# A decoder layer on one core: the attention's weighted sums in two parts, a norm and two casts moved to GpSimd

## The chip, the core and the metric

The kernel runs on one core of one Trainium2 chip. The metric is the device time of one execution in microseconds (us), median of three runs. All matrix products are made by TensorE (PE), from stationary weights that PE loads itself (PEld, beside the matmuls). VectorE (DVE), ScalarE (ACT) and GpSimd (POOL) work on rows of 128 partitions, SyncE (SP) issues the transfers.

## The reference, cut to what matters

For four sequences of 512 tokens of width 512, with a `_layernorm` after each of three parts:

```python
x = _layernorm(x + attn(x))          # 16 heads of 32, rope, causal softmax, then Wo
x = _layernorm(x + xattn(x, ctx))    # attention matrix made from ctx alone, 512x512, applied to x's columns
x = _layernorm(x + ffn(x))           # silu(gate) * up, 512 -> 2048 -> 512
# attn:   scores = q k^T / sqrt(32), causal;  out = softmax(scores) v
# xattn:  query, key = ctx Wq^T + bq, ctx Wk^T + bk (256 -> 128);  energy = query key^T;  x softmax(energy)^T
```

Everything is in float32 precision. Most products are made of three products of rounded halves (a high part `_hi` in the type fp32r and the rest `_lo`): hi x hi, lo x hi, hi x lo.

## The kernel before

The program is written out by engine, and each engine has one loop over the same numbered slots (`for t in range(BEGIN, END)`). What an engine does in slot t, and in which order, is fixed by tables; engines meet only at semaphores.

The attention takes 256 slots: 16 groups (four sequences by four groups of heads), 16 slots each (four heads by four blocks of 128 query rows). In slot t:

- PE makes the scores of tile t (L675, `ps`), then the pieces of other units that the table gives to this slot (`unit`, L660 for products, L658 for transposes: projections q, k, v, the output projection `o`, and from slot 224 on units of the cross attention: `c` context projections, `t` and `a` transposes, `e` energies, `m` mixing), then the transposes of the probabilities of tile t - 3 (L688, into `pa`, `pb`, `pc`).
- DVE takes the row maximum of tile t and writes `prob` (L1164); in other slots it moves `pb` and `pc` to `pT` (`move_b` L1171, `move_c` L1176).
- ACT takes the exponential of tile t (L902) and moves `pa` (`move_a` L909).

Scores of tile t wait for the row maximum of tile t - 2 (two buffers in PSUM); transposes of tile t wait for its exponential, and those into `pa` for the last `move_a`.

Once in a group, in its slot 20 (slots 20, 36, ... 244), and for the last group after the mixing unit `m1`, PE makes the weighted sums of the group (`weighted`, L703): 28 matmuls, each with a stationary block of only 32 columns (`tile_position`), four side by side in the array, which in the trace are 56 records:

```python
for moved in (a_moved, b_moved, c_moved):
    pe.wait_ge(moved, 4 * n + 4)
...
for k, s, count, at in WEIGHTED:
    for r in range(4):
        mm = pe.matmul(pv[D*r:D*r+D, s*P:(s+count)*P], vg[..][:, k, ..], pT[:, r, at*P:(at+count)*P], ..., tile_position=(0, D*r))
```

After it the reciprocals of the row sums are transposed (`r` unit), moved to `heads` by ACT (`move_r` L916) and multiplied in by DVE (`normalize` L1199).

The norm after attention: DVE sums and takes moments (`summed`, `moments`), POOL makes `rstd` and `nmr` (`root1`, L1513 to L1517), ACT applies them to a token tile (`layer_norm`, L922, `res<-res,nmr,rstd`). There are 16 token tiles, four in a batch (sequence). For a unit of the cross attention's context projection, ACT moves the result and adds the bias (`context_move`, L936), ACT casts its high half (`context_cast`, L941, `cqk_hi`), and POOL takes the low half (`context_query`, L1536, `cqk_lo`); the energies `e` wait for it. The table `CROSS` gives the first units of the cross attention their slots and PSUM banks; `hop` says how many slots behind the unit each step of its follow-up stands on the other engines. So a unit `a` (transposes of attention rows, L658 `pj<-ident,e`) in slot t has its `att_hi` on ACT (L952) in slot t + 1 and its `att_lo` on DVE (L1236) in slot t + 2, behind that slot's exponential, row maximum and moves.

After slot 256 the rest of the cross attention and the feed-forward part follow, which take from about 390 us to the end.

Of the kernel before, what the change touches and what calls it, by code (L numbers as in the profile page):

```python
# [18 lines left out]
ALU = mybir.AluOpType  # L19
# [8 lines left out]
ST = S // P  # L28
# [3 lines left out]
TILES = 16  # L32
# [13 lines left out]
GROUPS = B * G  # L46
# [7 lines left out]
AV, RECIPS, NORMALIZE, SPLIT_O = 20, 21, 25, 26  # L54
# [6 lines left out]

CROSS = [(("c", 0), 224, (6,), 0), (("c", 1), 228, (6,), 0), (("t", 0), 232, (4,), 1), (("e", 0), 234, (3,), 0),
# [3 lines left out]
CHAINS = ("m0:0 c2:3 c3:4 m1:1 AV r15:0 t4:5 t5:6 m2:7 e4:3 e5:4 m3:0 e6:1 e7:2 c4:5 c5:6 t6:7 t7:3 a4:4 a5:0 o12:1 a6:2 a7:5 o13:6 "  # L66
# [78 lines left out]
LAST_AV = ENDS["m", 1] + 1  # L145
# [11 lines left out]
def hop(key, k):  # L157

    return ENDS[key] + HOPS[key[0]][ENDS[key] >= SCORES][k]
# [7 lines left out]
def program(nc, ctx, d, out):  # L167
# [11 lines left out]
    with ExitStack() as first:  # L179
# [13 lines left out]
        res = sb("res", [P, ST, E], F32, first)  # L193
        oT_hi, oT_lo = sb("oT_hi", [P, G, S], F32R, first), sb("oT_lo", [P, G, S], F32R, first)
        o, rb = sb("heads", [P, S], F32, first), sb("rb", [P, ST, 4, D], F32, first)
# [62 lines left out]

    WEIGHTED = [(0, 0, 1, 6), (0, 1, 1, 8), (1, 1, 1, 9), (0, 2, 2, 0), (1, 2, 2, 2), (2, 2, 2, 4), (3, 3, 1, 7)]


    const_in, late_in = sem("const_in"), sem("late_in")
# [288 lines left out]
    def _(pe):  # L553
# [134 lines left out]
                mm = pe.transpose(dst[:, c:c + P], prob[:, t % PROBS, k * P:(k + 1) * P], ident[:])  # L688
            mm.then_inc(t_done, 1)

        def weighted(n):
            for moved in (a_moved, b_moved, c_moved):
                pe.wait_ge(moved, 4 * n + 4)
            pe.wait_ge(v_done, ST * (n // G) + ST)
            if n:
                pe.wait_ge(o_done, n)
            for key in BANKS[2]:
                if 0 < TILES * n + AV - STARTS[key] < TILES:
                    emptied(pe, key)
            for k, s, count, at in WEIGHTED:  # L700
                for r in range(4):
                    c = n % G * P + D * r
                    mm = pe.matmul(pv[D * r:D * r + D, s * P:(s + count) * P], vg[n // G % 2][:, k, c:c + D],  # L703
                                   pT[:, r, at * P:(at + count) * P], start=(k == 0), stop=(k == s + count - 1),
                                   tile_position=(0, D * r))
            mm.then_inc(av_done, 1)

        def three(dst, n, stationary, moving, first=True, final=True):

# [6 lines left out]
        for t in range(BEGIN, END):  # L716
            if 0 <= t < SCORES:
                scores(t)
            for key, start, counts, _ in UNITS:
                if start <= t < start + len(counts):  # L720
                    unit(key, sum(counts[:t - start]), counts[t - start])
            if 0 <= t - LAG < SCORES:
                transposes(t - LAG)
            for n in range(GROUPS):
                if t == (TILES * n + AV if n < GROUPS - 1 else LAST_AV):
                    weighted(n)

# [103 lines left out]
        h, c = NH - 1, NH // 2 - 1  # L831
# [26 lines left out]
    def _(act):  # L858
# [59 lines left out]
        def layer_norm(n):  # L918

            s = n % ST  # L920
            act.wait_ge(nmr_done, n + 1)
            act.activation(res[:, s, :], res[:, s, :], ACT.Identity, bias=nmr[:, s:s + 1], scale=rstd[:, s:s + 1]).then_inc(x1_done, 1)  # L922

        def context_half(b):
# [134 lines left out]
        for t in range(BEGIN, END):  # L1059
# [12 lines left out]
                    if t == ENDS["qk"[u], n] + SPLIT_QK:  # L1072
                        split_qk(n, u)
            for n in range(B * ST):
                if t == hop(("o", n), 3):
                    layer_norm(n)
            for (n, k), (at, _) in SPLIT_W.items():
                if t == at:
# [15 lines left out]
            for key in CONTEXT:  # L1094
                if key[0] == "c" and t == hop(key, 0):
                    context_move(key[1])
                if key[0] == "c" and t == hop(key, 1):
                    context_cast(key[1])
                if key[0] in "ta" and t == hop(key, 0):
                    t_half(*key)  # L1100
                if key[0] == "u" and t == hop(key, 0):
                    pair_input(key[1])
# [359 lines left out]
    def _(pool):  # L1462
# [46 lines left out]
        def root1(n):  # L1509

            s = n % ST
            pool.wait_ge(mv_done, n + 1)
            pool.tensor_scalar(veps[:, s:s + 1], mv[:, s, 1:2], EPS, None, ALU.add).then_inc(veps_done, 1)  # L1513
            pool.wait_ge(veps_done, n + 1)
            pool.tensor_tensor(rstd[:, s:s + 1], veps[:, s:s + 1], mhalf[:], ALU.pow).then_inc(rstd_done, 1)
            pool.wait_ge(rstd_done, n + 1)
            pool.tensor_scalar(nmr[:, s:s + 1], mv[:, s, 0:1], rstd[:, s:s + 1], -1.0, ALU.mult, ALU.mult).then_inc(nmr_done, 1)  # L1517

        def context_rest(b):
# [12 lines left out]
        def context_query(n):  # L1532

            hi, lo = cqk[n // 2 % 2]
            pool.wait_ge(cqkhi_done, n + 1)
            pool.tensor_tensor(lo[:, n % 2, :], c_raw[n // 2 % 2][:, n % 2, :], hi[:, n % 2, :].bitcast(F32),  # L1536
                               ALU.subtract).then_inc(cqklo_done, 1)
# [100 lines left out]
        for t in range(BEGIN, END):  # L1638
# [19 lines left out]
            if t >= 0 and b < B and at == (58 if b == B - 1 else 52):  # L1658
                residual(b)
            for key in CONTEXT:  # L1660
                if key[0] == "c" and t == hop(key, 2):
                    context_query(key[1])
                if key[0] == "e" and key[1] < KT and t == hop(key, 2):
                    energy_scale(key[1])
                if key[0] == "m" and key[1] < 2 * ST and t == hop(key, 1):
                    root(key[1])
# [82 lines left out]
```

## Time and profile before

| | |
|---|---|
| median of 3 runs | 970.6 us (970.26 to 971.39) |
| the profiled execution, its time | 968.91 us |
| its span, first to last instruction | 967.1 us |
| mean granted TensorE clock | 0.994 |
| busy: PE / PEld | 929.7 us (96%) / 756.2 us (78%) |
| busy: DVE / ACT / POOL | 733.9 (76%) / 514.9 (53%) / 598.2 us (62%) |

The profile's rows name an instruction by engine, source line, operation and `out<-in` tiles. A value in brackets is the time the engine sat idle just before it, and what ended that. Matmuls overlap each other in the rows: a 512-column matmul has 0.39 us, and the next one starts 0.23 us after it. Times are counted from the first instruction.

### The profile page before, as it was taken

What the parts mean: (1) busy time and instruction counts of PE and PEld (TensorE: products, weight loads), DVE (VectorE), ACT (ScalarE), POOL (GpSimd) and SP (SyncE); (2) the same over time, 40 slices, a digit from 0 to 9 for tenths busy, and PEclk for the clock granted to TensorE, in tenths of its full rate; (3) what the DMA queues carried; (4) which work ended last, traced back from release to release, by engine and by line L of the source; (5) the groups of instructions that cost most, each with busy time, mean ns of one, the idle gap of its engine ahead of it and who ended that gap; (6) DMA issues with size and microseconds to landing.
All of it is one profiled execution on the core that took longest, in us unless ns stands there. A gap on an engine that the chain in (4) does not pass through costs nothing.

```text
span 967.1 us, 16196 instructions
## 1 busy us (share of the span) xinstructions
PE 929.7 (96%) x5272; PEld 756.2 (78%) x5272; DVE 733.9 (76%) x1589; ACT 514.9 (53%) x1150; POOL 598.2 (62%) x645
## 2 busy tenths in 40 slices
PE   7888999999999978999999999999999999999997
PEld 5666888888788856887888888888878888888885
DVE  5667778678877876779478888867877888777777
ACT  4577777777877776566144443433534354333333
POOL 2467646745875546457466676777846786665644
PEclk9999999999999999999999999999999999999999
DMA  6986666965767780013102101111111113211102
GB/s 221 257 200 167 183 182 163 266 163 143 215 181 197 200 267 1 23 44 115 60 0 67 65 33 66 54 45 66 33 41 58 55 45 109 88 55 66 34 33 88
DMA packets 40883, 105.20 MB, mean 109 GB/s; under 512 B 4960, under 2 KB 5344, under 8 KB 38752
## 3 DMA queue, kind: packets, MB, share of 16 engines
q1 hardware_dynamic: 40800, 104.16, 36.7%
q8 instruction: 44, 0.72, 0.3%
q14 instruction: 39, 0.32, 0.1%
HBM read 78.98 MB, written 25.17 MB: 108 GB/s over the span
## 4 chain that ended last, share of the span: by engine, by line
PE 77%; DVE 6%; POOL 6%; ACT 5%; DMA 3%; issue 3%; SPq 0%; POOLq 0%; DVEq 0%; ACTq 0%
PE pd L712 27%; PE pj L660 14%; PE pj L712 10%; PE pg L712 5%; PE pu L712 5%; PE pv L703 3%; PE ps L675 3%; PE pa L688 2%; PE pb L688 2%; POOL raw L1466 1%; POOL raw L1475 1%; PE pc L688 1%; ACT e L946 1%; POOL raw L1471 1%; DMA qk_scratch<-raw 1%
## 5 line engine op out<-in xcount | busy, mean ns | idle before, releaser
L902 ACT ACTIVATE prob<-prob,nmax 128x512 f32<-128x512 f32 (+3 forms) x256 | 143.8, 562 | 72.9 <-DVE nmax L1164 71.8
L1164 DVE CUSTOM_DVE_ANT_0 prob<-ps,mask 128x512 f32<-128x512 f32 (+3 forms) x256 | 124.2, 487 | 72.5 <-PE ps L675 67.1
L675 PE MATMUL ps<-ks,qs 128*128 128x256 f32 (+2 forms) x256 | 104.9, 411 | 7.0 <-DVE nmax L1164 5.3
L1466 POOL TENSOR_TENSOR raw<-raw,cos 128x512 f32<-128x512 f32 x32 | 42.3, 1323 | 92.1 <-DVE pj L1146 76.5
L1633 POOL TENSOR_TENSOR g_lo<-gated,g_hi 128x512 fp32r<-128x512 f32 x32 | 46.3, 1448 | 79.7 <-ACT g_hi L1006 79.7
L1302 DVE TENSOR_TENSOR xb<-pd,xb 128x512 f32<-128x512 f32 x116 | 79.3, 684 | 19.6 <-PE pd L712 19.3
L1626 POOL TENSOR_TENSOR wop_lo<-wsum,wop_hi 128x512 fp32r<-128x512 f32 x64 | 81.6, 1299 | 1.4 <-ACT wop_hi L991 1.4
L712 PE MATMUL pd<-dn_hi,g_hi 128*128 128x512 f32 x244 | 75.4, 390 | 0.3 <-DVE x3T_lo L1250 0.3
L712 PE MATMUL pd<-dn_hi,g_lo 128*128 128x512 f32 x244 | 75.1, 389 | 0.0
L712 PE MATMUL pd<-dn_lo,g_hi 128*128 128x512 f32 x244 | 75.1, 389 | 0.0
L1606 POOL TENSOR_TENSOR wsum<-f_raw 128x256 f32<-128x256 f32 x32 | 23.7, 742 | 77.9 <-DMA f_raw<-in_w_ffn 77.7
L1006 ACT CAST g_hi<-gated 128x512 fp32r<-128x512 f32 x32 | 19.9, 622 | 91.0 <-DVE gated L1362 91.0
L991 ACT CAST wop_hi<-wsum 128x1024 fp32r<-128x1024 f32 x32 | 33.7, 1055 | 64.9 <-POOL wsum L1611 64.9
L675 PEld LDWEIGHTS ps<-ks,qs 128*128 128x128 f32 x256 | 48.8, 190 | 17.7 <-DVE nmax L1164 7.7
L660 PE MATMUL pj<-xT_hi,w_hi 128*128 128x512 f32 x128 | 51.9, 405 | 5.2 <-ACT xT_hi L872 5.1
L1475 POOL TENSOR_TENSOR raw<-raw,qk_hi 128x512 fp32r<-128x512 f32 x32 | 42.4, 1324 | 18.9 <-ACT qk_hi L896 18.9
L712 PEld LDWEIGHTS pd<-dn_hi,g_hi 128*128 128x128 f32 x244 | 45.6, 188 | 10.5 <-issue 0.7
L712 PEld LDWEIGHTS pd<-dn_hi,g_lo 128*128 128x128 f32 x244 | 45.8, 188 | 9.6
L712 PEld LDWEIGHTS pd<-dn_lo,g_hi 128*128 128x128 f32 x244 | 45.8, 188 | 9.5
L660 PE MATMUL pj<-xT_hi,w_lo 128*128 128x512 f32 x128 | 51.6, 403 | 1.5 <-DVE w_lo L1121 1.5
L660 PE MATMUL pj<-xT_lo,w_hi 128*128 128x512 f32 x128 | 51.4, 401 | 0.6 <-POOL xT_lo L1490 0.6
L688 PE MATMUL pb<-ident,prob 128*128 128x128 f32 x256 | 49.1, 274 | 0.1
(525 smaller groups left out, 2825.3 us busy)
## 6 DMA issues: line engine op xcount, KB each, us to landing
f_raw<-in_w_ffn SPq DMA_DIRECT2D x32, 768.0 KB, 4.2
qs<-qk_scratch SPq DMA_DIRECT2D x64, 256.0 KB, 4.8
ks<-qk_scratch SPq DMA_DIRECT2D x60, 256.0 KB, 7.3
qk_scratch<-qk_hi SPq DMA_DIRECT2D x32, 256.0 KB, 2.1
qk_scratch<-raw SPq DMA_DIRECT2D x32, 256.0 KB, 2.3
res<-in_x SPq DMA_DIRECT2D x4, 1024.0 KB, 5.0
x_scratch<-res SPq DMA_DIRECT2D x4, 1024.0 KB, 6.5
xb<-x_scratch SPq DMA_DIRECT2D x4, 1024.0 KB, 5.8
```

Source lines behind the costliest of these rows:

```text
L660: mm = pe.matmul(over[at], *pairs[i], start=i == 0, stop=i == len(pairs) - 1)
L675: pe.matmul(ps[:, t % 2, 0:w], qs[n % 2][:, r, s * P:(s + 1) * P], ks[n % 2][:, r, 0:w], start=True, stop=True).then_inc(s_done, 1)
L688: mm = pe.transpose(dst[:, c:c + P], prob[:, t % PROBS, k * P:(k + 1) * P], ident[:])
L712: mm = pe.matmul(dst, stationary(k)[a], moving(k)[c], start=(first and part == 0 and k == 0), stop=(final and part == 2 and k == n - 1))
L902: act.activation(prob[:, t % PROBS, 0:w], prob[:, t % PROBS, 0:w], ACT.Exp, bias=nmax[:, n % 2, i:i + 1], scale=-1.0, accum_out=rsum[:, n ...
L991: act.copy(wop_hi[h % 2][:, 3:7, :], wsum[:]).then_inc(wophi_done, 1)
L1164: dve.tensor_tensor_reduce(prob[:, t % PROBS, 0:w], ps[:, t % 2, 0:w], mask[:, S - w:S], -D ** -0.5, 3e38, ALU.add, ALU.min, accum_out=nma ...
L1302: dve.tensor_tensor(tile, pd[:, 2 + n % 2, :], tile, ALU.add).then_inc(part_added, 1)
L1466: pool.tensor_tensor(raw[:, u, :], raw[:, u, :], cos[:], ALU.mult).then_inc(cos_done, 1)
L1475: pool.tensor_tensor(raw[:, u, :].bitcast(F32R), raw[:, u, :], qk_hi[:, u, :].bitcast(F32), ALU.subtract).then_inc(qklo_done, 1)
L1626: pool.tensor_tensor(lo[:, 3 + k:5 + k, :], wsum[:, k:k + 2, :], hi[:, 3 + k:5 + k, :], ALU.subtract).then_inc(woplo_done, 1)
L1633: pool.tensor_tensor(lo, (gated, gated_b)[b][:], hi.bitcast(F32), ALU.subtract).then_inc((glo_done, glo_b_done)[b], 1)
```

## The change

Four edits:

1. `weighted` is cut in two. `weighted_ahead` stands at the end of the slot before (slot 19 of the group) and makes the first two entries of a reordered list, 8 matmuls of 256 columns; it waits for `a_moved` and `b_moved`, the values and the bank. `weighted` waits for `c_moved` and makes the other 20, in the slot in which all 28 stood. For the last group nothing stands between the two.
2. The unit `a0` goes from slot 243 to slot 244.
3. For batch 2 (token tiles 8 to 11), POOL applies the norm itself, with one instruction on 128x512 (`subtract`, `mult`) in `root1`, in the place of its `nmr`; ACT's `layer_norm` for these tiles is gone.
4. For context units 0 and 1, POOL casts the high half in `context_query`, which stands one slot earlier; ACT's cast is gone.

```diff
 CROSS = [...
-         (("e", 3), 241, (3,), 1), (("a", 0), 243, (4,), 0), ...
+         (("e", 3), 241, (3,), 1), (("a", 0), 244, (4,), 0), ...
...
-    WEIGHTED = [(0, 0, 1, 6), (0, 1, 1, 8), (1, 1, 1, 9), (0, 2, 2, 0), (1, 2, 2, 2), (2, 2, 2, 4), (3, 3, 1, 7)]
+    WEIGHTED = [(0, 2, 2, 0), (1, 2, 2, 2), (2, 2, 2, 4), (3, 3, 1, 7), (0, 0, 1, 6), (0, 1, 1, 8), (1, 1, 1, 9)]
...
-        def weighted(n):
-            for moved in (a_moved, b_moved, c_moved):
-                pe.wait_ge(moved, 4 * n + 4)
+        def weighted_ahead(n):
+            pe.wait_ge(a_moved, 4 * n + 4)
+            pe.wait_ge(b_moved, 4 * n + 4)
             pe.wait_ge(v_done, ST * (n // G) + ST)
             if n:
                 pe.wait_ge(o_done, n)
             for key in BANKS[2]:
                 if 0 < TILES * n + AV - STARTS[key] < TILES:
                     emptied(pe, key)
-            for k, s, count, at in WEIGHTED:
+            weighted_part(n, WEIGHTED[:2])
+
+        def weighted(n):
+            pe.wait_ge(c_moved, 4 * n + 4)
+            weighted_part(n, WEIGHTED[2:]).then_inc(av_done, 1)
+
+        def weighted_part(n, part):
+            for k, s, count, at in part:
...
-            mm.then_inc(av_done, 1)
+            return mm
...
             for n in range(GROUPS):
+                if t == (TILES * n + AV if n < GROUPS - 1 else LAST_AV) - 1:
+                    weighted_ahead(n)
                 if t == (TILES * n + AV if n < GROUPS - 1 else LAST_AV):
                     weighted(n)
...
         def layer_norm(n):
...
-            act.wait_ge(nmr_done, n + 1)
+            act.wait_ge(nmr_done, n + 1 - (ST if n >= 3 * ST else 0))
...
-                if t == hop(("o", n), 3):
+                if n // ST != 2 and t == hop(("o", n), 3):
                     layer_norm(n)
...
-                if key[0] == "c" and t == hop(key, 1):
+                if key[0] == "c" and key[1] >= 2 and t == hop(key, 1):
                     context_cast(key[1])
...
             pool.wait_ge(rstd_done, n + 1)
+            if n // ST == 2:
+                pool.tensor_scalar(res[:, s, :], res[:, s, :], mv[:, s, 0:1], rstd[:, s:s + 1], ALU.subtract, ALU.mult).then_inc(x1_done, 1)
+                return
...
             hi, lo = cqk[n // 2 % 2]
+            if n < 2:
+                pool.wait_ge(cqk_moved, n + 1)
+                pool.tensor_copy(hi[:, n, :], c_raw[0][:, n, :]).then_inc(cqkhi_done, 1)
             pool.wait_ge(cqkhi_done, n + 1)
...
-                if key[0] == "c" and t == hop(key, 2):
+                if key[0] == "c" and t == hop(key, 1 if key[1] < 2 else 2):
                     context_query(key[1])
```

PE in slots 242 to 244 (group 14), `pv` the bank of the weighted sums, `pj<-ident,e` the unit `a0`; `ps<-ks,qs` 128x256 is the scores of slot 243, 128x512 those of 244, 128x384 those of 245. Before:

```order
L675 MATMUL ps<-ks,qs 128x256
L658 MATMUL pj<-ident,e 128x128 x4
L688 MATMUL pa<-ident,prob 128x128 x4
L675 MATMUL ps<-ks,qs 128x512
L688 MATMUL pb<-ident,prob 128x128 x3
L703 MATMUL pv<-pT,vg 32x128 x12
L703 MATMUL pv<-pT,vg 32x256 x12
L703 MATMUL pv<-pT,vg 32x128 x4
L675 MATMUL ps<-ks,qs 128x384
```

and now:

```order
L675 MATMUL ps<-ks,qs 128x256
L688 MATMUL pa<-ident,prob 128x128 x4
L710 MATMUL pv<-pT,vg 32x256 x8
L675 MATMUL ps<-ks,qs 128x512
L658 MATMUL pj<-ident,e 128x128 x4
L688 MATMUL pb<-ident,prob 128x128 x3
L710 MATMUL pv<-pT,vg 32x256 x4
L710 MATMUL pv<-pT,vg 32x128 x16
L675 MATMUL ps<-ks,qs 128x384
```

Eight of the weighted sums' matmuls now stand between the transposes of slot 243 and the scores of slot 244, the other 20 where all 28 stood, and `a0` stands behind the scores of slot 244 and no longer ahead of slot 243's transposes. In groups 0 to 13 the same cut is made, without an `a0`.

ACT in slots 244 to 246; `att_hi` is the high half of `a0`, L902/L911 the exponential and L909/L918 the move of `pa`. Before:

```order
L902 ACTIVATE prob,rsum<-prob,nmax 128x512
L932 CAST c_hi<-c_raw 128x1024
L952 CAST att_hi<-pj 128x4x128
L902 ACTIVATE prob,rsum<-prob,nmax 128x384
L909 COPY pT<-pa 128x4x128
L902 ACTIVATE prob,rsum<-prob,nmax 128x128
```

and now:

```order
L911 ACTIVATE prob,rsum<-prob,nmax 128x512
L941 CAST c_hi<-c_raw 128x1024
L911 ACTIVATE prob,rsum<-prob,nmax 128x384
L918 COPY pT<-pa 128x4x128
L961 CAST att_hi<-pj 128x4x128
L911 ACTIVATE prob,rsum<-prob,nmax 128x128
```

`att_hi` of `a0` went from ahead of slot 245's exponential to behind it and behind the move of `pa`.

POOL in slots 225 to 228; `cqk` is context unit 0, the three rows ahead of it belong to token tile 10, and `oT` to the heads of group 12. Before:

```order
L1513 TENSOR_SCALAR veps<-mv 128x1
L1515 TENSOR_TENSOR rstd<-veps,mhalf 128x1
L1517 TENSOR_SCALAR nmr<-mv,rstd 128x1
L1536 TENSOR_TENSOR cqk_lo<-c_raw,cqk_hi 128x512
L1484 CAST oT_hi<-heads 128x512
L1486 TENSOR_TENSOR oT_lo<-heads,oT_hi 128x512
```

and now:

```order
L1522 TENSOR_SCALAR veps<-mv 128x1
L1524 TENSOR_TENSOR rstd<-veps,mhalf 128x1
L1527 TENSOR_SCALAR res<-res,mv,rstd 128x512
L1549 CAST cqk_hi<-c_raw 128x512
L1551 TENSOR_TENSOR cqk_lo<-c_raw,cqk_hi 128x512
L1493 CAST oT_hi<-heads 128x512
L1495 TENSOR_TENSOR oT_lo<-heads,oT_hi 128x512
```

The one-column `nmr` became the whole norm of a tile, and the cast stands ahead of `cqk_lo`.

## Rows read from the trace of the kernel before

**Rows 1.** busy time by stretch: us, PE, PEld, DVE, ACT, POOL, PEclk, DMA, GB/s

```profile
110.00:338.00 228.00, 227.53 (x1732) 185.32 (x1731) 179.77 (x565) 173.63 (x475) 140.56 (x138) 1.00 0.69 185
338.00:380.00 42.00, 32.30 (x269) 24.02 (x268) 30.25 (x95) 31.57 (x88) 24.39 (x21) 0.96 0.49 157
376.00:379.00 3.00, 2.92 (x9) 2.16 (x9) 1.37 (x4) 2.42 (x7) 2.17 (x2) 0.50 0.01 3
```

**Rows 2.** timeline of PE at group 6's weighted sums; start, us

```profile
187.75 0.49 PE L688 MATMUL pb<-ident,prob 128*128 128x128 f32 x3
188.18 2.38 PE L703 MATMUL pv<-pT,vg 128*32 128x128 f32 x56
190.48 0.45 PE L675 MATMUL ps<-ks,qs 128*128 128x384 f32 x1
190.76 0.39 PE L660 MATMUL pj<-xT_hi,w_hi 128*128 128x512 f32 x1
```

**Rows 3.** timeline of PEld there

```profile
188.17 2.11 PEld L703 LDWEIGHTS pv<-pT,vg 128*32 128x32 f32 x56 [0.17 <-issue]
190.48 0.19 PEld L675 LDWEIGHTS ps<-ks,qs 128*128 128x128 f32 x1 [0.20 <-issue]
```

**Rows 4.** timeline of PE, the same passage with no weighted sums between

```profile
94.45 0.49 PE L688 MATMUL pb<-ident,prob 128*128 128x128 f32 x3
...
94.95 0.39 PE L660 MATMUL pj<-wv_hi,xT_hi 128*128 128x512 f32 x1
```

**Rows 5.** instructions of L703 there: x, duration ns min/median/max, forms

```profile
L703 PE MATMUL pv<-pT,vg x56: 272/285/379, 188.2 to 190.3; 128*32 128x128 f32 x32, 128*32 128x256 f32 x24
```

**Rows 6.** timeline of PE behind group 1's weighted sums

```profile
87.18 0.50 PE L660 MATMUL pj<-xT_lo,w_hi 128*128 128x512 f32 x1 [0.37 <-POOL xT_lo L1490]
```

**Rows 7.** timeline of PE behind group 13's weighted sums

```profile
342.78 0.63 PE L688 MATMUL pa<-ident,prob 128*128 128x128 f32 x4 [0.92 <-ACT pT L909]
...
346.11 0.47 PE L660 MATMUL pj<-cqk_hi 128*128 128x512 f32 x1 [0.58 <-POOL cqk_lo L1536]
```

**Rows 8.** timeline of ACT there

```profile
343.97 0.63 ACT L941 CAST cqk_hi<-c_raw 128x512 fp32r<-128x512 f32 x1
...
344.99 0.81 ACT L922 ACTIVATE res<-res,nmr,rstd 128x512 f32<-128x512 f32 x1
...
346.40 0.61 ACT L902 ACTIVATE prob<-prob,nmax 128x384 f32<-128x384 f32 x1
```

**Rows 9.** timeline of DVE there

```profile
345.34 0.56 DVE L1164 CUSTOM_DVE_ANT_0 prob<-ps,mask 128x384 f32<-128x384 f32 x1 [0.96 <-PE ps L675]
```

**Rows 10.** timeline of POOL, a cast and a scaling of 128x512

```profile
346.57 0.61 POOL L1484 CAST oT_hi<-heads 128x512 fp32r<-128x512 f32 x1 [0.61 <-DVE heads L1199]
...
352.73 1.59 POOL L1542 TENSOR_SCALAR e<-e,erec 128x512 f32<-128x512 f32 x1 [4.18 <-DVE erec L1226]
```

**Rows 11.** timeline of PE around group 14's weighted sums

```profile
360.00 0.66 PE L658 MATMUL pj<-ident,e 128*128 128x128 f32 x4 [1.51 <-ACT e L946]
...
361.86 2.38 PE L703 MATMUL pv<-pT,vg 128*32 128x128 f32 x56 [0.21 <-issue]
364.16 0.44 PE L675 MATMUL ps<-ks,qs 128*128 128x384 f32 x1
...
365.87 0.65 PE L658 MATMUL pj<-ident,e 128*128 128x128 f32 x4 [0.22 <-DVE att_lo L1236]
```

**Rows 12.** timeline of ACT there

```profile
358.70 0.56 ACT L909 COPY pT<-pa 128x512 f32<-128x512 f32 x1
...
364.16 0.58 ACT L952 CAST att_hi<-pj 128x512 fp32r<-128x512 f32 x1
...
365.86 0.57 ACT L909 COPY pT<-pa 128x512 f32<-128x512 f32 x1
```

**Rows 13.** timeline of DVE there

```profile
361.23 0.42 DVE L1176 COPY pT<-pc 128x256 f32<-128x256 f32 x1
...
365.13 0.69 DVE L1236 TENSOR_TENSOR att_lo<-pj,att_hi 128x512 fp32r<-128x512 f32 x1
```

2 rows, old and new, of the table CROSS are left out of this document.

## Prediction

> **What bounds the kernel now.** I read busy time by stretch first. From 110 to 338 us, the dense part of the attention, PE is busy 227.53 of 228 us [rows 1]: nothing on DVE, ACT or POOL can win anything there, and whatever is added to PE is paid in full. From 338 to 380 us, where the first units of the cross attention stand among the last attention slots, PE is busy 32.30 of 42 us [rows 1]: 9.7 us of idle time, which only there something can give back. So the cut of the weighted sums, which is made in every group, is judged in the dense stretch, and what is taken off ACT in the other one.
>
> The timelines of PE and PEld at one group's weighted sums show what such a visit costs. The 56 records end without a gap inside, but PEld idles 0.17 us before the first weights and 0.20 us before the weights of the scores behind them, ended by no other engine [rows 3]. In all other places of this passage PEld loads ahead, beside the matmuls. The sum of starts agrees: from the transposes ahead to the product behind, 190.76 - 187.75 = 3.01 us [rows 2]; without a visit the same passage takes 94.95 - 94.45 = 0.50 us [rows 4]. The visit takes 2.51 us. Its columns need less: one record of 256 columns is 379 - 272 = 107 ns longer than one of 128 [rows 5], four run side by side, and 56 records are 14 quartets, 8 of 128 and 6 of 256 columns, 20 blocks of 128: 2.14 us. Left are 0.37 us of going into the 32-column form and out of it.
>
> **The change part by part.**
>
> *The cut, in the dense stretch.* It moves 8 of 28 matmuls a slot ahead and adds no matmul. It adds a second way in and out per group. The price of one pair lies between 0.20 us (only the gap behind is of the form, the gap ahead belongs to the semaphores waited for, of which the second part has one instead of several) and 0.37 us (both gaps). I take 0.35, near the upper end, since both gaps stand in PEld with no releaser and the columns' account leaves as much. The Trainium skill (TensorEngine Tiling (Array Packing), Key Properties) states that changing the tiling mode drains TensorE; by that rule both parts pay both gaps, and this term would be 11 x 0.37 = +4.1 us; where the gap ahead is the waits', it would be 11 x 0.20 = +2.2 us. Does the cut remove a wait in exchange? In the dense stretch there is none to remove: PE idles 0.47 us in 228.
>
> It is paid in groups 0 to 12, 13 times, less twice: behind group 1's weighted sums PE waits 0.37 us for `xT_lo` [rows 6], a chain of a transfer, an ACT cast and a POOL subtraction which began before; the same wait comes once more, behind group 9's. There the added 0.35 disappears in the wait. 11 x 0.35 = +3.85 us; with 0.20 +2.2, with 0.37 +4.1.
>
> *The norm of tiles 8 and 9 on POOL* falls in the dense stretch. ACT is busy 173.63 of 228 us there and not waited for: 0. On POOL one instruction of 128x512 with a scalar per row takes 1.59 us [rows 10] in place of a small one. POOL is busy 140.56 of 228 us [rows 1], which covers it; without that cover the queries and keys of group 15 would come up to 1.6 us late per tile.
>
> *Tiles 10 and 11 and the two casts* stand around 338 us. ACT loses the casts (0.63 us each) and two norms (0.81 each) [rows 8]. Those of tile 10 and unit 0 lie ahead of group 13's weighted sums, where ACT idles afterwards: 0. Behind them ACT is what PE waits for [rows 7], and 0.63 + 0.81, some 1.2 us because consecutive ACT instructions overlap a little, leave its queue. It can't use all: its exponential at 346.40 needs a row maximum that ends at 345.34 + 0.56 = 345.90, and that waited 0.96 us for PE [rows 8, 9]. So 0.50 us come forward, less the 0.35 that group 13's own second pair puts ahead of everything: about -0.1 net, from where the shape of before goes on. POOL's path to `cqk_lo` replaces an ACT cast, between other ACT work, by its own of 0.61 us [rows 10], right behind the moved unit; the wait of 0.58 us at 346.11 [rows 7] goes. What is late next there is `x1T_lo` on DVE, behind the same ACT chain. If nothing of the ACT relief came through, this part would be +0.35; if all of it, -1.2 + 0.35 = -0.85.
>
> *Group 14 and `a0`.* Before, `a0` waits to 360.00 for ACT's exponential of the energies, and slot 243's transposes and slot 244's scores queue behind it; then the weighted sums wait to 361.86 for DVE's `c` copy (361.23 + 0.42) [rows 11, 13]. Now the transposes can go at 358.70 + 0.56 = 359.3 [rows 12], and the first part (four blocks of 256 columns over two passes, 8 x 0.107 = 0.86, and 0.35) fills the hole up to about 360.9, where the scores of slot 244 stood before. `a0` (0.44) and the transposes (0.33) follow, and the second part starts without a wait at 362.1. The scores of slot 245 start at 363.5 instead of 364.16 [rows 11]: -0.65.
>
> But who waits for `a0`? Before, its `att_hi` stood on ACT at 364.16, ahead of slot 245's exponential; `att_lo` followed at 365.13 and ended at 365.82, and `a1` started at 365.87 [rows 11 to 13]. Now `att_hi` stands behind slot 245's exponential and behind the move of `pa`, both of which hang on the scores of slot 245. Before, that move ended at 365.86 + 0.57 = 366.43, 2.27 us after the scores started [rows 11, 12]; now at 363.5 + 2.3 = 365.8. `att_hi` ends at 366.3 to 366.4, `att_lo` (0.69) at 367.05, `a1` starts at 367.15 instead of 365.87: +1.3. Queued behind `a1` on PE are transposes into `pa` and the scores of slot 248, on DVE behind `att_lo` the row maximum of slot 247. The transposes had a small wait of their own behind `a1`, so a little less, I take +1.1, arrives at the scores of slot 248, and in front of the next waits nothing gives it back. From 0 (the delay falls into the waits that follow) to +1.3; the +1.1 stays.
>
> *Group 15* has no slot between its parts: only the order of its blocks changes, 0. The norm's and casts' other consequences (the store of batch 2 a little earlier) are waited for by nobody.
>
> **The sum:** +3.85 - 0.1 + 1.1 = +4.85 us on the profiled execution's own 968.9 us (span 967.1), that is 973.8. The median of the runs shown is 970.6, 1.7 above that execution; I add the difference to the median: **975.5 us**. With the ends of each term the sum goes from 2.2 - 0.85 + 0 = +1.35 to 4.1 + 0.35 + 1.3 = +5.75.
>
> **The rivals.** 0.2% is 1.9 us, about what a measurement of this kernel can tell from no change.
>
> *B, the second pair is (nearly) free.* The gaps could belong to the semaphores and the record keeping, and the second part could load its first weights beside the transposes. For it speaks only that no releaser is named; against it the columns' account. Time: 970.6 + 1.0 = 971.6, no change.
>
> *C, faster: the stall-rich stretch closes.* Place: 338 to 380 us, 9.7 us of PE idle. There each engine waits in turn for the last, so an earlier ACT and a second part that no longer waits could return at every later wait and not once. It has to give back 3.85 + 1.9 = 5.8 of the 9.7 us before the kernel is faster. With three quarters, 7.3: 970.6 + 3.85 - 7.3 = 967.2. Against it: of the listed waits the first two alone are ACT's casts and norms, and `a0`'s new place lengthens a chain.
>
> *D, TensorE's clock.* The granted clock is 0.50 from 376 to 379 us [rows 1], 1.2 instead of 2.4 GHz, behind the passage with the waits. PE is busy 2.92 us there; at full clock it would need half. One more such fall, or that one gone: 1.4 us either way, 976.9 or 974.1.
>
> *E, the change doesn't do what it says:* the first part could wait for `b_moved` in its slot. In group 14 `pb`'s copy is due before the hole ends, and elsewhere it comes before the next transposes; I give it no chance of its own.
>
> **How the numbers follow.** Forecast 0.60, its own range 973.5 to 977.5. B 0.12. C 0.08. D 0.20, half each way, both slower than before. So slower 0.80, same 0.12, faster 0.08. The range leaves out C and small tails: 971.0 to 978.0, from B and the lower ends of the terms to a clock fall on top.
>
> **What would show it.** Right: two visits of L710 in PE in each group 0 to 14, with 8 and 20 matmuls, and twice as many idle gaps of PEld of about 0.2 us before `pv` and before `ps`; a group in the dense stretch about 0.35 us longer from one weighted sum to the next; `cqk_lo` no longer waited for; the scores of slot 245 earlier relative to group 13's, but `a1` later behind them. Wrong: PEld without the second pair of gaps, or PE's idle time in the stretch of the crossover down from 9.7 us by more than 4.

## The result, and the profile after

| | before | after |
|---|---|---|
| median | 970.46 us (7 runs, 968.75 to 971.39) | 976.63 us (7 runs, 974.33 to 978.77) |
| ratio | | 1.0063, 95% interval 1.0047 to 1.0079 |
| profiled execution, its time / span | 968.91 / 967.1 us | 976.63 / 974.8 us |
| mean granted TensorE clock | 0.994 | 0.995 |
| busy: PE / PEld | 929.7 / 756.2 us | 934.4 / 756.1 us |
| busy: DVE / ACT / POOL | 733.9 / 514.9 / 598.2 us | 729.3 / 511.5 / 606.1 us |

The change made the kernel slower by 6.1 us (4.6 to 7.7), where 4.9 were forecast. PE has 4.7 us more busy time with the same matmuls. Part of it is that the profile counts the time around the weighted sums as busy (227.34 of 228 us in the dense stretch below); part can be the clock, for the run further down with all 28 matmuls in one piece has 933.1 us without any cut.

Busy time by stretch after (us; PE, PEld, DVE, ACT, POOL; granted clock; DMA; GB/s), for [rows 1]:

```profile
110.00:338.00 228.00, 227.34 (x1717) 181.90 (x1716) 176.27 (x555) 170.13 (x468) 140.57 (x133) 1.00 0.67 178
338.00:380.00 42.00, 34.79 (x277) 27.09 (x275) 29.71 (x96) 28.46 (x81) 24.39 (x22) 0.92 0.63 203
360.00:364.00 4.00, 3.99 (x16) 3.60 (x17) 3.93 (x14) 2.83 (x10) 2.14 (x2) 0.57 0.89 352
374.00:377.00 3.00, 3.00 (x15) 2.82 (x14) 0.82 (x3) 0.96 (x3) 0.00 (x0) 0.50 0.00 0
```

PE is as full in the dense stretch as before, but its records there are 1717 where they were 1732: it is slower, not idle. Between 338 and 380 us its idle time fell from 9.7 to 7.2 us, but that is no gain: the work in this window has moved by 6 us, and two stretches at half clock stand there (before one), in which four transposes into `pa` are busy 1.06 us instead of 0.60.

PE after, at group 6's weighted sums (start, us), for [rows 2]:

```profile
190.12 0.60 PE L688 MATMUL pa<-ident,prob 128*128 128x128 f32 x4
190.65 1.07 PE L710 MATMUL pv<-pT,vg 128*32 128x256 f32 x16
191.65 0.50 PE L675 MATMUL ps<-ks,qs 128*128 128x512 f32 x1
...
192.69 0.49 PE L688 MATMUL pb<-ident,prob 128*128 128x128 f32 x3
193.11 1.51 PE L710 MATMUL pv<-pT,vg 128*32 128x256 f32 x40
194.55 0.44 PE L675 MATMUL ps<-ks,qs 128*128 128x384 f32 x1
```

And PEld, for [rows 3]:

```profile
190.65 0.59 PEld L710 LDWEIGHTS pv<-pT,vg 128*32 128x32 f32 x16 [0.17 <-issue]
191.65 0.19 PEld L675 LDWEIGHTS ps<-ks,qs 128*128 128x128 f32 x1 [0.41 <-issue]
...
193.10 1.24 PEld L710 LDWEIGHTS pv<-pT,vg 128*32 128x32 f32 x40 [0.17 <-issue]
194.55 0.19 PEld L675 LDWEIGHTS ps<-ks,qs 128*128 128x128 f32 x1 [0.20 <-issue]
```

Both parts have a gap ahead and a gap behind. The gap behind the first part reads 0.41 and not 0.20 us. The blocks that end there have 256 columns, and PE may still be at work on them when PEld has loaded their weights; that is argued, not shown. A dearer change of form it is not, as the sum of starts shows. From the first record to the next instruction the two parts take 191.65 - 190.65 = 1.00 and 194.55 - 193.11 = 1.44 us. Before, all 56 records took 190.48 - 188.18 = 2.30 us [rows 2], so the two parts take 0.14 us more. The rest of the price is ahead of the added visit: the transposes into `pa` start 0.53 us before it (190.12 to 190.65), where before they started 0.36 us ahead of the scores:

```profile
186.38 0.60 PE L688 MATMUL pa<-ident,prob 128*128 128x128 f32 x4
186.74 0.48 PE L675 MATMUL ps<-ks,qs 128*128 128x512 f32 x1
```

These are 0.17 us; 0.14 + 0.17 = 0.31, and from one group to the next 0.33 are measured.

**Where the time went.** Each matmul of PE was set against the same one before, and the shift between them followed from the start:

- 1.7 us are there at 45 us, ahead of the first weighted sums. The change does not touch what stands ahead of that, and every other traced execution is late there too against this one of before, by 0.6 to 1.8 us, with a cut or without. So this is a matter of the single execution that was profiled.
- From group 0 to group 12 the shift grows at each weighted sum, by 0.33 us in most: the scores behind the sums stand at 86.79 instead of 84.54 in group 1 (+2.25), at 194.55 instead of 190.48 in group 6 (+4.07), at 301.55 instead of 296.26 in group 11 (+5.29). The period of a group is 301.55 - 280.15 = 21.40 us, before 296.26 - 275.19 = 21.07. 13 such steps are 4.3 us. In these two executions they come to 3.95: 0.37 are lost once behind group 9, in a wait for `xT_lo`, 0.17 around 75 us, where before has a fall of the clock and after has none, and 0.14 are added by a longer wait behind group 1.
- Between groups 12 and 13, a new stall: the shift goes up by 0.77.
- Group 13 adds 0.36, the energies' wait for `cqk_lo` gives 0.69 back.
- The next transposes into `pa`, which hang on ACT, take 0.23 of these 0.69 again: the shift behind them is 6.32.
- Around group 14 the shift rises by 1.41, to the end. `a1` is 1.26 later than what comes in. In the run with tiles 8 and 9 normed on ACT, where no fall of the clock stands near, 1.03 of the same 1.26 last (3.77 us of shift ahead, 4.80 behind). The other 0.38 are the clock: the falls at 360 and 374 us after against the one at 376 before.

1.7 + 3.95 + 0.77 + 0.36 - 0.69 + 0.23 + 1.41 = 7.7 us, the difference of the spans.

The wait behind group 9 is nothing that a cut takes in. Of the 13 executions with a trace only that of the kernel before has it:

```profile
256.13 0.50 PE L660 MATMUL pj<-xT_lo,w_hi 128*128 128x512 f32 x1 [0.21 <-POOL xT_lo L1490]
```

In the run of the new order in one piece, without a cut, the same product starts at 255.90 with no wait. So the cut costs its 0.33 us in each of the 13 groups, 4.3 us, and against an execution without that wait and with the clock set aside the terms are 4.3 + 0.77 - 0.10 + 1.03 = 6.0 us; the medians say 6.1.

The new stall: PE waits for the move of `pa`.

```profile
326.64 0.63 PE L688 MATMUL pa<-ident,prob 128*128 128x128 f32 x4 [0.40 <-ACT pT L918]
```

The exponential ahead of that move, and the move, on ACT:

```profile
325.32 0.61 ACT L911 ACTIVATE prob<-prob,nmax 128x384 f32<-128x384 f32 x1 [2.73 <-DVE nmax L1173]
...
325.93 0.56 ACT L918 COPY pT<-pa 128x512 f32<-128x512 f32 x1
```

The row maximum for which the exponential waits, on DVE, and what stands ahead of it:

```profile
321.94 2.02 DVE L1202 COPY rb<-rrec 128x512 f32<-128x512 f32 x1
...
324.72 0.56 DVE L1173 CUSTOM_DVE_ANT_0 prob<-ps,mask 128x384 f32<-128x384 f32 x1
```

POOL at that time:

```profile
318.00 2.10 POOL L1527 TENSOR_SCALAR res<-res,mv,rstd 128x512 f32<-128x512 f32 x1
...
321.30 2.38 POOL L1541 TENSOR_TENSOR c_lo<-c_raw,c_hi 128x1024 fp32r<-128x1024 f32 x1
```

Read from the bottom: the norm of token tile 8, the first of the four on POOL, takes 2.10 us, so `c_lo` starts only at 321.30, behind one more subtraction, and runs when DVE's copy of the reciprocals, `rb`, is issued. The copy takes 2.02 us, the row maximum behind it is late, and so are the exponential and the move.

### The profile page after: what moved, and what is told of

Its sections match the earlier page's. It is cut to its first block, busy times and chain, and to the rows that moved or that the text cites. A ratio compares the mean times of both kernels' runs of the same rounds, so it can differ in the third digit from the quotient of the medians.

```text
span 974.8 us, 16190 instructions
## 1 busy us (share of the span) xinstructions
PE 934.4 (96%) x5272; PEld 756.1 (78%) x5272; DVE 729.3 (75%) x1589; ACT 511.5 (52%) x1144; POOL 606.1 (62%) x647
## 4 chain that ended last, share of the span: by engine, by line
PE 78%; DVE 6%; ACT 5%; POOL 4%; DMA 3%; issue 2%; SPq 0%; POOLq 0%; DVEq 0%; ACTq 0%
PE pd L719 27%; PE pj L660 14%; PE pj L719 10%; PE pg L719 5%; PE pu L719 5%; PE ps L675 4%; PE pv L710 4%; PE pa L688 2%; PE pb L688 2%; POOL raw L1475 1%; DMA qk_scratch<-raw 1%; PE pc L688 1%; ACT e L955 1%; PE pj L658 1%; POOL raw L1480 1%
## 5 line engine op out<-in xcount | busy, mean ns | idle before, releaser
L911 ACT ACTIVATE prob<-prob,nmax 128x512 f32<-128x512 f32 (+3 forms) x256 | 143.8, 562 | 84.1 <-DVE nmax L1173 83.2
```

The lines of the kernel that those rows point to most:

```text
L911: act.activation(prob[:, t % PROBS, 0:w], prob[:, t % PROBS, 0:w], ACT.Exp, bias=nmax[:, n % 2, i:i + 1], scale=-1.0, accum_out=rsum[:, n ...
```

## The experiments

All were timed in rounds beside runs of the kernel before on the same chip. Ratios are to those.

### Two theories and what would tell them apart

One theory is the prediction's: each further visit to the 32-column form costs a pair of gaps, about 0.33 us, whatever it waits for, and around group 14 the new place of `a0` costs. The rivals: the cost comes of the order of the blocks or of the wait in the middle; the cost comes of the work moved to POOL; the cut in group 14 costs and not `a0`.

### The cut alone, groups 0 to 13

```diff
+    CUT = (0, 1, 2, 3, 4, 5, 6, 7, 8, 9, 10, 11, 12, 13)
...
+                if n in CUT and t == TILES * n + AV - 1:
+                    weighted_ahead(n)
```

> The kernel before with the cut alone, in groups 0 to 13 (group 14 and a0 as before, no work moved to POOL). Theory (each way into and out of the 32-column form costs 0.33 us of PE, as the trace after shows from one group to the next): 13 groups in the dense stretch less one or two absorbed in the wait for xT_lo, 0 to 0.35 for group 13: +3.7 to +4.4 us. Rival (the cut is free, the 6 us come from POOL's work and from group 14): +0.5 us or less.

Measured: 975.43 us, ratio 1.0055 (1.0034 to 1.0076): +5.3 us (3.3 to 7.4). In its trace the period of a group is 278.96 - 257.56 = 21.40 us as in the changed kernel. The growth per group is 0.31 to 0.35 us. Its span is 4.4 us longer than that of before, but 1.3 of them stand there at 45 us; the shift grows by 3.15 us up to group 12, since behind groups 1 and 9 the waits for `xT_lo` of that one execution are missing here (0.5 and 0.37 us). They are missing without a cut too: up to the same place five uncut kernels (the moves to POOL twice, tiles 10 and 11 with the casts, the new order in one piece, group 14 and `a0`) win 1.0 to 1.2 us on that execution. Against them the cut costs 4.1 to 4.3 us, 13 times 0.32 to 0.33. The cut alone makes most of the whole difference of 6.1.

### A third visit per group

Against the kernel of the cut alone:

```diff
             pe.wait_ge(c_moved, 4 * n + 4)
-            weighted_part(n, WEIGHTED[2:]).then_inc(av_done, 1)
+            weighted_part(n, WEIGHTED[3 if n in CUT else 2:]).then_inc(av_done, 1)
...
+            for n in CUT:
+                if t == TILES * n + AV:
+                    weighted_part(n, WEIGHTED[2:3])
             if 0 <= t - LAG < SCORES:
                 transposes(t - LAG)
```

> As the run with the cut in groups 0 to 13, with a third visit in each of these groups (the third entry alone, ahead of slot 20's transposes). Nothing else moves. Theory (a visit costs 0.33 us of TensorE however small its part): one group to the next 21.7 us in the dense stretch, against 21.07 before and 21.4 with two parts; +8 to +9.5 us against before. Rival (the cost is of the slot in which the first part stands, or of the semaphores): a third part behind the same semaphores adds nothing, +5 us as with two parts.

Measured: 979.1 us, ratio 1.0096 (1.0078 to 1.0115), +9.3 us (7.5 to 11.1) for two further visits in 14 groups, 28 visits: 0.33 us each. The period is 284.08 - 262.39 = 21.69 us, 0.62 over that of before, 0.31 per visit. PEld at group 6, the middle part:

```profile
195.26 0.16 PEld L713 LDWEIGHTS pv<-pT,vg 128*32 128x32 f32 x8 [0.37 <-issue]
195.83 0.31 PEld L689 LDWEIGHTS pb<-ident,prob 128*128 128x128 f32 x3 [0.41 <-issue]
```

The middle part waits for nothing that the first had not waited for, and has both gaps all the same. The price goes with the number of visits, not with their length and not with their waits.

### The new order with a wait in the middle, but in one piece

```diff
+    CUT = ()
...
+        def weighted(n):
+            if n not in CUT:
+                weighted_ahead(n)
+            pe.wait_ge(c_moved, 4 * n + 4)
+            weighted_part(n, WEIGHTED[2:]).then_inc(av_done, 1)
```

> The kernel before with the new order of the blocks and with the wait for c_moved between block 2 and 3, but all 28 matmuls in one slot, in all groups. Theory (the price is of changing form, not of waiting): 2.31 us from the first weighted sum to the scores behind, as before, and 0 us in all (within 0.2%). Rival (the semaphore wait in the middle is the price): +0.2 us or more a group, +3 us.

`weighted_ahead` waits for `a_moved` and `b_moved` and makes the first two blocks, as in the change. Measured: 970.03 us, ratio 0.9995 (0.9982 to 1.0008). PE and PEld at group 6:

```profile
188.26 2.38 PE L713 MATMUL pv<-pT,vg 128*32 128x256 f32 x56
```

```profile
188.26 2.11 PEld L713 LDWEIGHTS pv<-pT,vg 128*32 128x32 f32 x56 [0.17 <-issue]
190.56 0.19 PEld L676 LDWEIGHTS ps<-ks,qs 128*128 128x128 f32 x1 [0.20 <-issue]
```

The same 2.38 and 2.11 us as before, in another order and with a wait between. The 56 records stand without a gap inside, so the semaphore was there when it was waited for: neither the order nor such a wait costs anything that can be measured.

### Only the moves to POOL, twice

`weighted` and `a0` stay as before; of the change only these two parts are made, with ACT's instructions gone:

```diff
+            if n in (8, 9, 10, 11):
+                pool.tensor_scalar(res[:, s, :], res[:, s, :], mv[:, s, 0:1], rstd[:, s:s + 1], ALU.subtract, ALU.mult).then_inc(x1_done, 1)
+                return
...
+            if n in (0, 1):
+                pool.wait_ge(cqk_moved, n + 1)
+                pool.tensor_copy(hi[:, n, :], c_raw[0][:, n, :]).then_inc(cqkhi_done, 1)
```

> The kernel before with the norm of batch 2 and the casts of context units 0 and 1 on POOL, no cut. Theory 1 (ACT's relief is worth 0.1 to 0.5 us behind group 13, and the row copy on DVE that POOL's longer queue now holds up costs 0.5 us behind group 12): between -0.3 and +0.4 us. Theory 2 (relief closes idle time at every later wait of the stretch): -1.2 us or better.

Measured: 968.91 us, ratio 0.9989 (0.9976 to 1.0001). The trace shows the energies' wait for `cqk_lo` gone, which brings their start forward by 0.70 us; 0.22 go again at the next transposes into `pa`, and 0.48 last. There is no new stall at 320 us. Since this was the fastest of all, it was run again:

> The kernel before with only the two moves to POOL (norm of tiles 8 to 11, casts of units 0 and 1), a second time and beside the kernels of this call. Theory 1: the wait for cqk_lo goes and 0.8 us come back, 969.6 us, ratio 0.9985 to 0.9995. Theory 2: the first run's 0.9989 was chance, ratio 0.9995 to 1.0010.

Measured: 970.47 us, ratio 1.0000 (0.9988 to 1.0012). In the trace 0.69 us come back at the same place and 0.46 last; in the time nothing is left that can be told from no change. No version was found that beats the kernel before.

### The moves to POOL in parts

First only the norm of tiles 8 to 11 (the first piece of the diff above). Then the norm of tiles 10 and 11 with the two casts: `if n in (10, 11)` in the first piece, and the second piece.

> The kernel before with the norm of batch 2's four tiles on POOL alone, casts on ACT. Theory (ACT loses one norm behind group 13, and the context casts stay): half of what both together gave, -0.6 us. Rival 1 (GpSimd's 2.1 us instruction holds DVE's copy of the reciprocals up and costs as much as it gives): 0. Rival 2 (all of the gain of 1.2 us is the norm's): -1.2 us.

Measured: 969.25 us, ratio 0.9991 (0.9980 to 1.0001).

> The kernel before with both casts on POOL and the norm of tiles 10 and 11 alone; tiles 8 and 9, in the dense stretch, stay on ACT. Theory (the norms of tiles 8 and 9 bring nothing and lie in front of POOL's long subtraction beside DVE's copy): -1.2 us or a little better. Rival (they mattered): 0.3 us or more worse than all four tiles on POOL.

Measured: 969.77 us, ratio 1.0004 (0.9989 to 1.0018). By the times neither part costs or gives anything that can be told from nothing; they exclude a cost of 2 us. The traces say more. With the norm alone the energies still wait 0.57 us for `cqk_lo`, and yet 0.46 us come forward at the next product, as many as last with both parts and with the second one (0.46). What the two runs have in common is the norm of tiles 10 and 11: the casts on POOL end a wait, and add nothing that lasts.

### The changed kernel with tiles 8 and 9 normed on ACT again

```diff
-            if n // ST == 2:
+            if n in (10, 11):
                 pool.tensor_scalar(res[:, s, :], res[:, s, :], mv[:, s, 0:1], rstd[:, s:s + 1], ALU.subtract, ALU.mult).then_inc(x1_done, 1)
```

> The changed kernel with the norm of token tiles 8 and 9 back on ACT; tiles 10 and 11 and the casts stay on POOL. Theory 1 (the norm of tile 9, 2.10 us on POOL, pushed POOL's c_lo onto the copy of the reciprocals on DVE, and that made the new stall of 0.57 us ahead of slot 212's transposes into pa): c_lo ends before that copy starts, the copy takes 0.43 us, PE does not wait there, 976.6 - 0.6 = 976.0 us. Theory 2 (the stall comes of the cut, whatever POOL does): PE waits 0.4 to 0.6 us there again and the time stays at 976.6. The medians alone can hardly tell 0.6 us; the trace between 318 and 328 us does.

Measured: 974.90 us, ratio 1.0058 (1.0041 to 1.0075), which overlaps that of the changed kernel, as was to be expected of so little. The trace decides. DVE, POOL and PE at that place:

```profile
320.20 0.43 DVE L1205 COPY rb<-rrec 128x512 f32<-128x512 f32 x1
```

```profile
317.71 2.39 POOL L1544 TENSOR_TENSOR c_lo<-c_raw,c_hi 128x1024 fp32r<-128x1024 f32 x1
```

```profile
324.35 0.60 PE L689 MATMUL pa<-ident,prob 128*128 128x128 f32 x4
```

`c_lo` ends at 320.10, the copy is issued at 320.20 and takes 0.43 us, and the transposes into `pa` don't wait. The new stall of the changed kernel comes of the norm of tile 8, by way of `c_lo` and `rb`. (The expectation above names tile 9. Tile 9's norm runs only at 325.87 in the changed kernel, behind the late row maximum; this run takes both back.)

It takes the cut too. With the norms on POOL but without the cut the copy fell 0.56 us ahead of `c_lo` (315.26 against 315.82), took 0.88 us, and PE had no such stall. In the changed kernel it is issued 0.64 us behind the start of `c_lo`. The 1.2 us between the two match what the first part puts ahead of the scores behind whose row maximum the copy stands: 0.86 us of columns by the account of the prediction, and 0.33. The run with the cut alone has no stall there, and that with `a0` back in slot 243, which has the cut and the norms, has the same stall, 0.78 us.

### Group 14 and `a0`: both, `a0` back, the cut alone

First the kernel before with group 14 cut and `a0` in slot 244:

```diff
-         (("e", 3), 241, (3,), 1), (("a", 0), 243, (4,), 0), ...
+         (("e", 3), 241, (3,), 1), (("a", 0), 244, (4,), 0), ...
...
+    CUT = (14,)
```

> The kernel before with the cut in group 14 alone and a0 in slot 244. Theory (att_hi of a0 falls behind slot 245's exponential and delays a1): +1.0 to +1.6 us. Rival (the first part fills the hole in which PE waited for a0, and the rest follows earlier): -0.5 us.

Measured: 972.26 us, ratio 1.0018 (1.0002 to 1.0034): +1.7 us (0.2 to 3.3).

Then the changed kernel with `a0` in slot 243 again:

```diff
-         (("e", 3), 241, (3,), 1), (("a", 0), 244, (4,), 0), ...
+         (("e", 3), 241, (3,), 1), (("a", 0), 243, (4,), 0), ...
```

> The changed kernel with a0 back in slot 243, ahead of the first part of group 14. Theory (a0 in 243 holds the first part up until ACT's exponential of the energies, a0 in 244 holds a1 up; the two prices are near each other): +5 to +7 us against before, as the changed kernel. Rival (a0's new place is most of the crossover's loss): 1.2 us less than the changed kernel, some +5.

Measured: 974.97 us, ratio 1.0042 (1.0029 to 1.0056), some 2 us under the changed kernel.

Last the kernel before with only `CUT = (14,)`, `a0` left in slot 243:

> The kernel before with the weighted sums of group 14 alone cut in two; the unit a0 stays in slot 243. Theory 1 (a0's new slot is what costs around group 14, and not the cut): a1 keeps its att_lo, the cut costs at most one visit, +0.3 us, and may give back up to 0.6 us of the wait for the c copy: 969.8 to 970.7 us against 970.4, no difference that can be measured, and in the trace a1 within 0.4 us of the kernel before. Theory 2 (the cut in this group costs by itself, because it stands ahead of the scores of slot 244): +1.7 us as in the run with a0 moved too, 972.1 us, and the scores of slot 245 later than before.

Measured: 970.29 us, ratio 0.9997 (0.9984 to 1.0009).

So the cut is nearly free in this one group, and `a0`'s slot is what costs. The wait of `a1` shows it. PE in the changed kernel, for [rows 11]:

```profile
365.77 0.63 PE L688 MATMUL pa<-ident,prob 128*128 128x128 f32 x4 [0.92 <-ACT pT L918]
366.33 1.07 PE L710 MATMUL pv<-pT,vg 128*32 128x256 f32 x16
...
367.67 0.60 PE L658 MATMUL pj<-ident,e 128*128 128x128 f32 x4
...
368.52 1.51 PE L710 MATMUL pv<-pT,vg 128*32 128x256 f32 x40
369.97 0.45 PE L675 MATMUL ps<-ks,qs 128*128 128x384 f32 x1
...
373.50 0.91 PE L658 MATMUL pj<-ident,e 128*128 128x128 f32 x4 [2.04 <-DVE att_lo L1245]
```

With `a0` back in slot 243:

```profile
371.32 0.66 PE L658 MATMUL pj<-ident,e 128*128 128x128 f32 x4 [0.60 <-DVE att_lo L1245]
```

And with only group 14 cut:

```profile
362.96 1.51 PE L713 MATMUL pv<-pT,vg 128*32 128x256 f32 x40
364.41 0.44 PE L676 MATMUL ps<-ks,qs 128*128 128x384 f32 x1
...
366.49 0.66 PE L659 MATMUL pj<-ident,e 128*128 128x128 f32 x4 [0.60 <-DVE att_lo L1248]
```

The wait is 2.04 us with `a0` in slot 244 and 0.60 in slot 243, before 0.22 [rows 11]. ACT and DVE of the changed kernel show what is in it, for [rows 12, 13]:

```profile
371.05 0.62 ACT L911 ACTIVATE prob<-prob,nmax 128x384 f32<-128x384 f32 x1 [0.43 <-DVE nmax L1173]
...
371.67 0.56 ACT L918 COPY pT<-pa 128x512 f32<-128x512 f32 x1
372.13 0.59 ACT L961 CAST att_hi<-pj 128x512 fp32r<-128x512 f32 x1
```

```profile
372.75 0.69 DVE L1245 TENSOR_TENSOR att_lo<-pj,att_hi 128x512 fp32r<-128x512 f32 x1 [0.73 <-ACT att_hi L961]
```

`att_hi` stands behind the exponential of slot 245 and the move of `pa`, and `att_lo` waits 0.73 us for it.

With only group 14 cut, the scores of slot 245 start at 364.41 where they started at 364.16 before, and that execution came in 0.19 us late: 0.06 us for the cut. The hole in which PE waited for the `c` copy takes in the rest of the 0.33 us. It does not give back more, because the first part stands ahead of the scores of slot 244, which start at 362.21 and not at 360.84. Their exponential on ACT is late by this, and `att_hi` behind it, so `a1` waits 0.60 us even with `a0` in its old slot. It is 0.43 us late, of which 0.21 last. In the run with `a0` back the same 0.21 last (5.01 us of shift ahead, 5.22 behind), against 1.03 with both edits: `a0`'s slot is worth 0.8 us in the traces.

## Why the prediction was right, and where it was off

The forecast was slower, 975.5 us, and 976.6 us were measured, inside its own range of 973.5 to 977.5. The mechanism of the cut, of the relief of ACT and of `a0` was the forecast one. But the 6.1 us lie beyond the 5.75 to which the prediction's terms add up with each at its end; the range held them because it had room for a fall of the clock, and what filled it was a stall that no term had. That it held is in part luck.

- **Dense stretch, the cut: the price right, the two absorptions wrong.** 0.35 us per pair were taken, and 0.33 measured, by the period of a group, by the cut alone, and by the third visit. The waits for `xT_lo` come and go from one execution to the next, cut or not: that behind group 9 is in none but the one read, and that behind group 1 is 0.37 to 0.62 us in five of the thirteen traces, 0.51 in the change, and missing in the other eight. They belong to that execution and are no cover: 3.85 us were summed, and 13 x 0.33 = 4.3 is what the cut costs. Rival B, a second pair that is nearly free, fell with the cut alone. The 0.20 us of the lower bound, by which the gap ahead belongs to the waits, fell with the third visit, which has both gaps and no wait of its own. The Trainium skill (TensorEngine Tiling (Array Packing), Key Properties) says that a change of the tiling mode drains TensorE. The third visit agrees, with 0.31 us for a part of two quartets that waits for nothing.
- **Norm of tiles 8 and 9 on POOL, costed at nothing: wrong.** This is the step that failed. The cover was read as an average: POOL is busy 140.56 of 228 us. What counted was who stands behind the norm in POOL's queue and what that meets. The instruction takes 2.10 us, not the 1.59 of the nearest row, which makes one operation per element and not two. With the norm of tile 8 ahead of it and the cut's 1.2 us ahead of the copy, `c_lo` met DVE's `rb`, and 0.40 us of wait were seen at 326.64, 0.77 us of shift until group 13. The prediction named a late group 15 as the cost without cover; that did not happen.
- **Tiles 10 and 11, the casts, group 13: right.** -0.1 net was forecast. +0.36 for the visit, -0.69 for the wait that is gone and +0.23 at the transposes behind it are -0.10. 0.50 us of ACT's relief were to come through, and 0.46 to 0.48 did, in all seven kernels that have these two norms on POOL. That the casts are part of it was not so: the norm alone gives as much. The energies no longer wait:

```profile
352.20 0.47 PE L660 MATMUL pj<-cqk_hi 128*128 128x512 f32 x1
```

```profile
350.07 0.61 POOL L1549 CAST cqk_hi<-c_raw 128x512 fp32r<-128x512 f32 x1 [0.46 <-ACT c_raw L945]
350.77 1.28 POOL L1551 TENSOR_TENSOR cqk_lo<-c_raw,cqk_hi 128x512 fp32r<-128x512 f32 x1
```

  POOL's low half ends at 352.05, 0.15 us ahead of its user.
- **Group 14 and `a0`: right in both halves.** Against the shift of 6.37 us with which the trace comes into this place, the scores of slot 245 are 0.56 us earlier (forecast 0.65) and `a1` is 1.26 us later (forecast 1.3). +1.1 was taken for what lasts, and 1.03 last where no fall of the clock blurs it. The two runs that part the edits add what the forecast did not say: the cut alone is +0.43 at `a1` and +0.21 behind it, so that `a0`'s slot makes 0.8 of the 1.03. By the medians `a0`'s slot is worth about 2 us, with a spread that holds 0.8 too; what is over 0.8 in it stays open.
- **Rival C, the stretch closes and the kernel is faster: wrong.** It needed 5.8 us of the 9.7 us of idle time. The two things that could give anything gave 0.69 and 0.56, and both went again in part or whole at the next wait.
- **Rival D, a clock fall more or less:** one more is what happened in the profiled execution. Two stretches at 0.5, near 360 and 374 us, stand against one at 376 before. In other kernels of this study they stand elsewhere or are missing. In the run of group 14 and `a0` one fell on the first part of the weighted sums and cost 1.6 us; the one at 376 us before cost 1.1 against the run with `a0` back, which has none there. The one at 360 us after cost 0.05, because the wait behind it takes it in. So a fall moves a single execution by nothing to 1.6 us, by where it meets PE. Net, the clock is 0.38 of the 7.7 us between the two spans, and no run ties it to the change.
- **The size.** 4.85 were summed and 6.1 measured. The four terms differ from theirs by +0.45 (the cut, whose two absorptions were none), +0.77 (the unforeseen stall), 0 (moves behind group 13) and -0.07 (group 14 and `a0`): 4.85 + 1.15 = 6.0 us. That this comes so near to 6.1 says little, since the medians leave 4.6 to 7.7.

## What to carry to other kernels

Count how often TensorE changes between the 128-column and the 32-column form before work of the narrow form is cut up to fit gaps: where the engine is full, every further visit costs a third of a microsecond. Even where the added part filled a wait, as in one group of 15 here, nothing was won. Before a wait in a trace is counted as cover, look for it in a second execution: two were counted here that most executions don't have. When work goes to an engine with idle time, read not its busy share but the instructions queued behind the new one, and which copies on DVE they will now meet. A unit moved by a slot takes its follow-up on the other engines with it: look for what stands ahead of that follow-up in the new slot.

## What was not expected of the hardware

DVE's copy of 128x512 between two tiles in SBUF takes 0.43 us alone, and as long as POOL is busy plus 0.28 us where a POOL instruction runs already. In the kernel before:

```profile
315.44 1.39 DVE L1193 COPY rb<-rrec 128x512 f32<-128x512 f32 x1
```

```profile
314.14 2.41 POOL L1529 TENSOR_TENSOR c_lo<-c_raw,c_hi 128x1024 fp32r<-128x1024 f32 x1
```

`c_lo` ends at 314.14 + 2.41 = 316.55 and the copy at 316.83. In the changed kernel `c_lo` ends at 323.68 and the copy at 323.96: 0.28 us behind in both, though one copy waited 1.11 and the other 1.74 us. In the run with only the norms on POOL the copy ends at 318.60, again 0.28 us behind a POOL instruction. It is so in all 13 traces: of 208 such copies, 98 start while a POOL instruction runs, and all but one of these end 0.28 to 0.31 us behind it; the 109 that meet none take 0.43 us. The Trainium skill (SBUF — State Buffer, Who interferes with whom) says that a copy can take the port pair that DVE shares with GpSimd, and that whoever issues first has it for its whole instruction while the other is fully blocked. These ends agree. That it is this pair, and not something else the two share, no run here shows. A row maximum, which reads its scores from PSUM, is not held up: in the run with tiles 8 and 9 normed on ACT one of 128x512 runs at 319.30 beside `c_lo` and has its 0.69 us.

A POOL instruction with two operations and two scalars per row takes 2.10 us on 128x512, the same in every run (2.09 to 2.10), and with one operation and one scalar 1.59 [rows 10]: half a microsecond for the second operation and the second scalar together. Which of the two makes it, no run here parts.
